# A two-layer convolution kernel: norms with fewer linked steps, another order of VectorE's work, and first pieces that move between engines

## The reference, cut to what matters

```python
# layer 0 (x: 4 x 256 x 64 x 64)
k = conv(x, w1, 7x7, dilation 2, pad 6) + b1            # 256 -> 128 channels
k = conv(k, w2, 1x1) + b2                               # 128 -> 49
attn = softmax(k, axis=1)
x = einsum('bkchw,bkhw->bchw', shifts(x, 49), attn)     # 49 shifted copies, weighted per pixel
# layer 1
h = relu(bn(conv(x, v1, 1x1), g1, c1))                  # 256 -> 64
h = relu(bn(conv(h, v2, 3x3, pad 1), g2, c2))           # 64 -> 64
h = bn(conv(h, v3, 1x1), g3, c3)                        # 64 -> 256
out = relu(h + x)
# bn: mean and variance over batch and pixels, then gamma * (x - mean) / sqrt(var + 1e-5) + beta
```

## Time and profile before

| what | value |
|---|---|
| three runs | 822.93, 823.03, 823.52 us; median 823.03 |
| profiled execution | 823.48 us, its span 821.6 us |
| TensorE busy (matmul) | 787.4 us, 96% of the span |
| VectorE, ScalarE, GpSimd busy | 661.3, 381.8, 353.3 us |
| mean granted clock of TensorE | 0.99 of full |

### The profile page before, as it was taken

How to read it: one execution, slowest core, us unless ns; L and a number is a source line. 1 busy time by engine, 2 the same in 40 slices (tenths; PEclk the granted TensorE clock), 3 DMA queues, 4 the chain that set the end, 5 groups by cost and what they waited for, 6 DMA issues and landing times.

```text
span 821.6 us, 13841 instructions
## 1 busy us (share of the span) xinstructions
PE 787.4 (96%) x4990; PEld 722.5 (88%) x4990; DVE 661.3 (80%) x908; ACT 381.8 (46%) x665; POOL 353.3 (43%) x255
## 2 busy tenths in 40 slices
PE   6989988999999999999999999999998989999996
PEld 2369988999999999999999999999997877777785
DVE  5998998896789689869967896898558766977796
ACT  3632212443453434534434534335336767717497
POOL 3345663483277248525832772385120014415300
PEclk9999999999999999999999999999999989999999
DMA  9951237948894997699588949766877999305398
GB/s 311 326 173 23 53 81 191 242 128 216 181 252 102 246 175 210 167 208 215 133 221 173 252 109 239 157 172 173 194 154 233 284 262 378 133 1 198 148 421 359
DMA packets 250108, 162.17 MB, mean 197 GB/s; under 512 B 191881, under 2 KB 232826, under 8 KB 247226
## 3 DMA queue, kind: packets, MB, share of 16 engines
q1 hardware_dynamic: 241050, 141.31, 65.9%
q10 hardware_dynamic: 8992, 19.99, 7.5%
HBM read 99.48 MB, written 56.36 MB: 190 GB/s over the span
## 4 chain that ended last, share of the span: by engine, by line
PE 73%; DVE 11%; issue 5%; DMA 4%; POOL 3%; ACT 3%; SPq 0%; DVEq 0%; ACTq 0%; POOLq 0%
PE ps L1313 20%; PE ps L1315 20%; PE ps L1314 20%; PE ps L1430 4%; PE ps L1446 3%; PE ps L1480 3%; POOL ring L865 2%; DVE whole L1829 2%; DMA x_dram<-x 1%; DVE logit L1922 1%; DVE wsum L1779 1%; DMA xbuf<-in_x 1%; PE ps L1691 1%; DVE wpart L1779 1%; POOL whole L860 1%
## 5 line engine op out<-in xcount | busy, mean ns | idle before, releaser
L865 POOL TENSOR_TENSOR ring<-whole,ring 128x576 fp32r<-128x576 f32 x112 | 194.1, 1739 | 280.0 <-ACT ring L948 280.0
L1313 PE MATMUL ps<-w_hi,ring 128*128 128x336 f32 x832 | 276.4, 332 | 3.5 <-POOL ring L865 3.5
L1315 PE MATMUL ps<-w_hi,ring 128*128 128x336 f32 x832 | 263.5, 317 | 0.0
L1314 PE MATMUL ps<-w_lo,ring 128*128 128x336 f32 x832 | 262.3, 315 | 0.0
L1313 PEld LDWEIGHTS ps<-w_hi,ring 128*128 128x128 f32 x832 | 158.3, 190 | 9.7 <-issue 6.1
L1314 PEld LDWEIGHTS ps<-w_lo,ring 128*128 128x128 f32 x832 | 158.1, 190 | 0.0
L1315 PEld LDWEIGHTS ps<-w_hi,ring 128*128 128x128 f32 x832 | 157.2, 189 | 0.0
L948 ACT ACTIVATE ring<-whole 128x576 fp32r<-128x576 f32 x112 | 87.1, 782 | 93.8 <-POOL whole L860 52.7
L948 ACT ACTIVATE band_hi<-ps 128x320 fp32r<-128x320 f32 (+1 forms) x128 | 53.1, 418 | 126.8 <-PE ps L1430 119.2
L1313 PE MATMUL ps<-band_hi,xT_hi 128*128 128x224 f32 (+2 forms) x320 | 94.6, 296 | 1.6 <-DVE xT_lo L1732 1.2
L1314 PE MATMUL ps<-band_lo,xT_hi 128*128 128x224 f32 (+2 forms) x320 | 92.3, 288 | 0.0
(11 more groups left out here) (222 smaller groups left out, 1370.9 us busy)
## 6 DMA issues: line engine op xcount, KB each, us to landing
xq<-in_x SPq DMA_DIRECT2D x108, 256.0 KB, 4.7
raw<-bands SPq DMA_DIRECT2D x32, 768.0 KB, 6.8
xbuf<-in_x SPq DMA_DIRECT2D x16, 1024.0 KB, 8.9
x_dram<-x ACTq DMA_DIRECT2D x32, 512.0 KB, 5.7
bands<-wide SPq DMA_DIRECT2D x64, 199.0 KB, 5.0
x1in<-x_dram SPq DMA_DIRECT2D x6, 2048.0 KB, 15.9
out<-x1in SPq DMA_DIRECT2D x12, 1024.0 KB, 4.5
bands<-wide SPq DMA_DIRECT2D x3, 1792.0 KB, 11.3
```

The lines of the kernel that those rows point to most:

```text
L865: pool.tensor_tensor(split(k, 1), positions(whole[:, k % TBUFS, :], 0, 2), split(k, 0).bitcast(F32), ALU.subtract).then_inc(sig_lo_done, 1)
L1313: pe.matmul(dst, l_hi, r_hi_, start=first, stop=False, **kw)
L1314: pe.matmul(dst, l_hi, r_lo_, start=False, stop=False, **kw)
L1315: return pe.matmul(dst, l_lo, r_hi_, start=False, stop=last, **kw)
```

## The change

- **Second pair (VectorE).** `a_of(3)` and `b_of(3)` stand ahead of the last five combines of pair 0 instead of behind them; `signal(20)` ahead of `softmax_top(0)`. In `half(3)` one HALF1 combine moves from part 4 to part 6 and the other two to part 5, behind the first bands.
- **Behind the convolution.** `y_out` is split into `y_add` and `y_stat`; `y_add(g-1, 1)` moves ahead of `xT(g, 2)` and `bandlo(g, 4)`, `y_stat` behind `bandlo(g, 4)`. `xT(13, 0)` moves ahead of the last `softmax_end`, `softmax_max` behind `xT(12, 3)` and `xT(13, 3)`. ScalarE's `x_out(12, 0)` moves behind `xT`.
- **Last projection.** The last half image is projected with eight products of 64 columns that sum in PSUM, so that neither `yhalf` nor the add is needed; `bn_stats` reads PSUM, and ScalarE copies the result out afterwards. Its x goes to DRAM from SyncE's queue instead of ScalarE's, and nine of the thirteen `load_y` are issued behind it.
- **Norms.** EPS and a factor 2 go into the root's bias and scale; the root reads PSUM in BN1; mean*gamma is done beside the root; shift is one instruction from -mean*gamma; scale and shift are not linked. BN2 averages mean and variance in one product. In BN3 the means' products come ahead of the covariance's, and `last(0)` is cut in two around the sums.
- **First pieces.** `step` and `step_lo` of piece 0 move from GpSimd to VectorE; the copies of v3 (`prepare_last`) come behind them; the ReLU of the edge rows of piece 2 moves into piece 1. Dummies: 14 become 9; behind BN2 four `center` products and 5 dummies instead of 16.

The diff, cut to its core:

```diff
@@ SyncE
             store_y(DRAIN)
             load_v()
-            for i in range(STEPS - LAG):
+            for i in range(4):
                 load_y(i)
             store_y(DRAIN + 1)
+            sp.wait_ge(x1_done, 4 * STEPS)
+            sp.dma_start(x1_dram[STEPS - 1][:, :, HALF:SPX].rearrange("b p e -> p b e"),
+                         x1_2[:, :, :]).then_inc(x1_stored[1], 16)
             store_y(DRAIN + 2)
+            for i in range(4, STEPS - LAG):
+                load_y(i)
@@ ScalarE
             prepare(0)
-            yhalf(STEPS - 1, 1)
             x_out(STEPS - 1, 1)
+            act.wait_ge(y1_stat, 2 * STEPS)
+            copy(y1_of(STEPS - 1)[:, 1, :], turn_bank("proj", STEPS - 1, 1)[0:MID1, :]).then_inc(y1_last, 1)
             prepare(1)
-            root(1, BN1_ROOT)
+            act.wait_ge(eps_set, 1)
+            act.wait_ge(bn_pe, 1)
+            root(mv[:, 8:9], ps[:, 7, 0:1], 2.0)
+            for a in range(2):
+                rows = slice(64 * a, 64 * a + 64)
+                copy(v3_hi[rows, a, :], psR[1][rows, C:2 * C]).then_inc(v_hi_done, 1)
@@ ScalarE, h1_part
+                if p != 2:
+                    edges(p)
                 main(0)
...
+                if p == 1:
+                    edges(2)
                 act.wait_ge(left_done, p + 1)
@@ TensorE
-            proj(STEPS - 1, 1)
+            last_proj()
             prepare(1)
...
-            for i in range(14):
+            for i in range(9):
                 pe.matmul(ps[:, spare, 0:P], ident[:, :], ident[:, :], start=True, stop=True)
-            pe.wait_ge(v_lo_done, 8)
-            pe.wait_ge(v_hi_done, 8)
-            pe.wait_ge(vT_done, 2)
+            pe.wait_ge(v_lo_done, 6)
+            pe.wait_ge(v_hi_done, 6)
             pe.wait_ge(borders, 2)
...
             warm(10)
-            average(BN2_MEAN, 0)
-            average(BN2_VAR, 4)
-            warm(16)
+            pe.wait_ge(bn_dve, BN2_MEAN)
+            pe.matmul(ps[:, 7, 0:2], gavg[:, :], mv[:, 0:2], start=True, stop=True).then_inc(bn_pe, 1)
...
+            for k in range(4):
+                centre(k)
+            warm(5)
...
-            last(0)
+            pe.wait_ge(bn_dve, BN3_MEAN)
+            for cb in range(CB):
+                mm = pe.matmul(ps[:, 6, 2 * cb:2 * cb + 2], vT[:, cb * P:(cb + 1) * P], gm[:, 0:2], start=True, stop=True)
+            mm.then_inc(means_ps, 1)
             pe.wait_ge(bn_dve, BN3_COV)
             pe.matmul(ps[:, 3, 0:C], cov[:, :], vT[:, :], start=True, stop=True).then_inc(quad_ps, 1)
-            last(1)
+            last(0, 0)
             pe.wait_ge(bn_dve, BN3_QUAD)
...
             mm.then_inc(sums_ps, 1)
-            for m in range(2, 32):
+            last(0, 1)
+            for m in range(1, 32):
                 last(m)
@@ VectorE, drain
                 bandlo(g, 3)
+                y_add(g - 1, 1)
                 if g > DRAIN:
                     xT(g, 2)
                 bandlo(g, 4)
-                y_out(g - 1, 1)
+                y_stat(g - 1, 1)
@@ VectorE, second pair
                 signal(17)
+                a_of(3)
+                b_of(3)
                 for i in range(C_MHALF + 1, COMBOS):
                     combine(0, i)
-                a_of(3)
-                b_of(3)
                 c_of(2)
+                signal(20)
                 softmax_top(0)
-                signal(20)
                 signal(21)
@@ VectorE, affine
-                link(dve.tensor_scalar(mv[:, 6:8], var, EPS, None, ALU.add))
+                link(dve.tensor_tensor(mv[:, 12:12 + width], mv[:, 2:2 + width], gamma, ALU.mult))
                 dve.wait_ge(bn_act, roots)
-                link(dve.reciprocal(mv[:, 10:12], mv[:, 8:10]))
-                link(dve.tensor_tensor(sc, mv[:, 10:10 + width], gamma, ALU.mult))
-                link(dve.tensor_tensor(mv[:, 12:12 + width], mean, sc, ALU.mult))
-                link(dve.tensor_tensor(sh, beta, mv[:, 12:12 + width], ALU.subtract))
+                link(dve.reciprocal(mv[:, 10:10 + width], mv[:, 8:8 + width]))
+                dve.tensor_tensor(scale[:, i:i + width], mv[:, 10:10 + width], gamma, ALU.mult).then_inc(bn_dve, 1)
+                for j in range(width):
+                    dve.scalar_tensor_tensor(out=shift[:, i + j:i + j + 1], in0=mv[:, 10 + j:11 + j], scalar=mv[:, 12 + j:13 + j],
+                                             in1=beta[:, j:j + 1], op0=ALU.mult, op1=ALU.add).then_inc(bn_dve, 1)
```

More of the change, by code:

```diff
@@ L516, in turn_bank_at @@
             return turns[turn_of[kind, g, i]][3]
+        BN1_MEAN = [b for b in (2, 5, 6) if b not in [turn_bank_at(*t) for t in (("band", STEPS - 1, NT - 1), ("band", STEPS - 1, NT - 2),
+                                                                                ("proj", STEPS - 1, 1))]][0]
         def x_count(g, pt):
@@ L1100, in image_part @@
                     x_hi(image, 0)
-                    x_out(image, 0)
+                    if image < DRAIN - 1:
+                        x_out(image, 0)
                 if part == 12:
@@ L1192, in _, with edges @@
             act.wait_ge(unit_done, len(UNITS) * STEPS)
-            def h1_part(p):
+            def edges(p):
                 n, r0, r1 = PIECES[p]
-                if n >= 2:
-                    act.wait_ge(c2_done, 6 * (n - 1))
-                def main(b):
-                    part = yin[:, 2 * n + b, max(r0, 1):min(r1, SH), :]
-                    act.activation(part, part, ACT.Relu, bias=shift[:, 0:1], scale=scale[:, 0:1]).then_inc(relu1, 1)
                 def edge_row(a, r):
@@ L1219, in h1_part, with main, high @@
                     edge_row(1, SH)
+            def h1_part(p):
+                n, r0, r1 = PIECES[p]
+                if n >= 2:
+                    act.wait_ge(c2_done, 6 * (n - 1))
+                def main(b):
+                    part = yin[:, 2 * n + b, max(r0, 1):min(r1, SH), :]
+                    act.activation(part, part, ACT.Relu, bias=shift[:, 0:1], scale=scale[:, 0:1]).then_inc(relu1, 1)
+                def high(dst, src):
+                    copy(dst, src).then_inc(h1_hi_done, 1)
+                if p != 2:
+                    edges(p)
                 main(0)
@@ L1261, in _ @@
                 c2_copy(j)
-            root(2, BN2_ROOT)
+            act.wait_ge(bn_dve, BN2_ROOT)
+            root(mv[:, 8:9], mv[:, 5:6])
             act.wait_ge(bn_dve, BN2_END)
@@ L1291, in _ @@
             upper(15)
-            root(3, BN3_ROOT)
+            act.wait_ge(bn_dve, BN3_ROOT)
+            root(mv[:, 8:10], gm[:, 12:14])
             act.wait_ge(bn_dve, BN3_END)
@@ L1708, in last @@
                 for b in range(2):
+                    if part == 1 - b:
+                        continue
                     sub = 2 * n + b
@@ L2190, in _ @@
             link(dve.bn_aggr(mv[0:MID1, 0:2], stats1[:, :, :].rearrange("p k e -> p (k e)")))
+            dve.memset(sums[:, 15:16], EPS).then_inc(eps_set, 1)
             dve.wait_ge(bn_loaded, 16 * 12)
@@ L2210, in h1_part @@
                 minus(odd_lo[:, at, r0:r1, :], odd, odd_hi[:, at, r0:r1, :].bitcast(F32)).then_inc(odd_lo_done, 1)
+                if not p:
+                    minus(step[:, r0:r1, :], odd, even).then_inc(step_done, 1)
                 dve.wait_ge(left_edge, p + 1)
@@ L2213, in h1_part @@
                 minus(left_lo[:, at, r0:r1, :], left[:, r0:r1, :], left_hi[:, at, r0:r1, :].bitcast(F32)).then_inc(left_lo_done, 1)
+                if not p:
+                    dve.wait_ge(step_done, 1)
+                    dve.wait_ge(h1_hi_done, STEP + 1)
+                    minus(step_lo[:, at, r0:r1, :], step[:, r0:r1, :], step_hi[:, at, r0:r1, :].bitcast(F32)).then_inc(step_lo_done, 1)
+                    prepare_last()
             def c2_out(j):
```

174 lines of the change are left out of this document (97 added, 77 removed).

## The result

The changed kernel takes 818.11 us (median of 6 runs, 817.34 to 821.49); the kernel before, on the same chip, 823.27 (6 runs, 822.70 to 824.91). The ratio is 0.9941, with an interval of 0.9923 to 0.9960: 5 us faster, where 9 were forecast, and inside the forecast's range by 0.4 us. The profiled execution took 817.85, its span 816.0.

A forecast was written before the change was run, and what follows sets the result against it. A different owner per stage: VectorE in the second pair, first drained images and Gram stage, TensorE in the last. Terms -1.5 - 1.5 - 3.2 - 0.5 - 2.5 + 0.3 = -8.9 led to 814.2 us; range 811.0 to 818.5.

The forecast's parts named there:

- Second pair: Images 2 and 3, 100 to 160 us: reordering VectorE's list makes it net 1.5 us shorter.
- Bounds: 0, if GpSimd's instructions collide with others instead: Second pair: worst case of the -1.5 term, no gain if GpSimd's instructions collide with other ones; best case -3.8.
- For which TensorE then waits a little over 1 us; hidden: Second pair: TensorE waits for ScalarE's late rounding of chunk 20, at no cost, being ahead of VectorE.
- nothing more: Reordering in `half(3)`: removes TensorE's 1.7 us wait but gains no time, as VectorE's later list keeps its length.
- Drained images: Behind the convolution: the earlier `y_add` frees the bank before TensorE asks, saving twice 0.7 us; -1.5.
- Last projection and BN1: Between the convolutions: earlier aggregation, an earlier root and a ScalarE not held by the x store give -3.2 us.
- Rival B: BN1: the x store lands as late as before, ScalarE stays held, gain 1.1 instead of 3.2; 816.3 us; chance 0.12.
- Loads moved behind: Nine y loads, a y store and the last x store, issued later, still arrive in time: 0, bounds 0 and +5.
- First pieces: Start of the second convolution: TensorE's first wait for `odd_lo`, 0.7, goes, the second stays set by ScalarE; -0.5 us.
- BN2: Second norm: shorter chain and fewer dummies bring VectorE's first transposed block from 746.84 to 744.35; -2.5 us.
- BN3: Last stage: TensorE owns it; its new order takes 7.85 us to `last(4)` where it took 7.55; +0.3.
- Rival A: Second pair gains 0 and a low clock in the first pieces costs 1.8 us: 817.5 us; chance 0.2.

The follow-up runs named there:

- 1: The changed kernel with both moves of VectorE's second pair put back (`a_of(3)`/`b_of(3)` and `signal(20)`); ratio 0.9941 to the kernel before.
- 4: The kernel before with only VectorE's new order of the second pair (both moves), nothing else of the change; ratio 1.0014 to the kernel before.
- 2: The changed kernel with only `signal(20)` put back behind `softmax_top`; ratio 0.9923 to the kernel before.
- 3: The changed kernel with only `a_of(3)` and `b_of(3)` put back behind the combines; ratio 0.9947 to the kernel before.
- 5: The changed kernel with ScalarE rounding chunk 20 ahead of pair 0's exponentials instead of behind them; ratio 0.9922 to the kernel before.
- 6: The changed kernel with the combines in `half(3)` put back to their old slots; ratio 0.9947 to the kernel before.
- 9: The changed kernel with `last(0)`'s first half ahead of BN3's means and its second ahead of the sums; ratio 0.9931 to the kernel before.
- 11: The changed kernel with VectorE's old second-pair order and `last(0)`'s halves ahead of BN3's means and sums; ratio 0.9919 to the kernel before.
- 12: The changed kernel with the old second-pair order, `last(0)`'s halves ahead of BN3's means and sums, and `softmax_end(0)` ahead of `signal(21)`; ratio 0.9894, median 815.01 us.
- 7: The changed kernel with all 13 y loads issued in one go again, ahead of the last stores; ratio 0.9966 to the kernel before.
- 8: The changed kernel with 16 dummy products instead of 5 between BN2's averages and the first transposes; ratio 0.9970 to the kernel before.
- 10: The changed kernel without the nine dummies between BN1's averages and the first pieces; ratio 0.9976 to the kernel before.

## Why the prediction was right and where it was not

**The range and the figure.** 818.11 lies inside 811.0 to 818.5, 0.4 from its upper end; the central figure, 814.2, missed it by 3.9. Most stages came out by the steps given. The second pair did not, and one of the prediction's own signs of being wrong came: TensorE's waits as long in sum as before (4.7 for 4.6) and VectorE no earlier.

**Second pair, forecast -1.5, measured +1.2: the step that failed.** The text said that the stretching of `signal(21)` (1.2) and the idle 1.32 before it go. Both went: 0.76 and no wait for GpSimd. It also said that there would be a wait of about 1.0 for the copied rows, with `c_of` and `signal(20)` in front of it; the two take 2.1 longer than it took them for and fill it. GpSimd's signal for chunk 18 was to start 3.8 earlier; counted from `signal(17)` it started 1.3 earlier (108.28 for 109.41), since `a_of` and `b_of` were stretched by 2.2. What it left out is that moved instructions get in GpSimd's way at their new place. VectorE lost 1.1 at `a_of`, 1.1 at `b_of`, 1.0 at `c_of`, 1.05 at `signal(20)` and 1.1 at `wide`: 5.3, against 0.9 + 1.0 + 1.2 saved at the first softmax addition, the subtraction and `signal(21)` and 1.3 of idle time, 4.4. That gives +0.9 of the 1.2. A new idle 0.34 for the exponentials and a `me` that is 0.35 shorter cancel; the remaining 0.3 lies in the hand-overs between instructions. "Bounds: 0, if GpSimd's instructions collide with others instead" saw the mechanism, but took it to be no worse than an even trade, for which it had no reason. The upper bound should have counted each of the moved instructions as meeting one ring step: three of 1.1 are +3.3 against the -1.5. Experiments 1 and 4 show the sign and the size, 2 and 3 that the two moves do not add up.

**Where the wait went.** "For which TensorE then waits a little over 1 us; hidden": the wait was 3.0, since the exponentials came 3.5 later, and it was hidden (5). The reordering in `half(3)`: "nothing more" is right (6); the wait came from another operand.

**Drained images, -1.5:** -1.46. No wait of 0.7 is left from 636 to 660. That the figure agrees this well is in part luck: of the twelve traces with this change seven have 55.9 to 56.1 for the piece, and 3, 6, 9, 11 and 12 have 56.5 to 58.0, where before it was 57.37. In 9, 11 and 12 TensorE waited 1.3, 1.8 and 1.4 for the landing of the bands, and without that they have 56.2; for 3 and 6 the cause stays open.

**Last projection and BN1, -3.2:** -3.35, by the steps given: aggregation at 671.04 (forecast 671.1), root 672.59 (672.65), ReLU 1.07 behind it (1.15). Rival B is refuted for the kernel as changed, and 7 shows its condition: with the loads together ScalarE is held till 672.1, and the gain up to `even_hi` is 1.1 (8.81 for 9.92), as that rival said. The store landed at 666.1, by 666 as forecast. By the rule quoted there (the Trainium skill, DMA: Bandwidth & Descriptors, Queues, rings and completion order) a DMA engine takes turns between the queue rows that have work. The prediction read it as saying that queued loads cost the store little, which the rule does not say; the rows show 12.0 to 12.3 against 4.7 to 6.2, and whether turns alone give that no run here shows.

**Loads moved behind, 0:** no wait for them in the trace.

**First pieces -0.5, BN2 -2.5:** -0.76 and -2.34, to the aggregate's start and from it. That the dummies would have hidden the shorter chain is shown by 8.

**BN3, +0.3:** +0.46 to the fifth tile (8.12 for 7.66, from 767.78 to the 775.44 of the earlier trace rows), for the reason given, and 9 takes it back and 0.26 more. The +0.3 itself rests on a slip: the terms listed add up to 7.65, not 7.85, which would be +0.1 over 7.55. From the first means' product they took 7.88 (761.55 to 769.43), each term a little more than its estimate. Of the +0.9 to the end, 0.4 lies behind the fifth tile, less than the scatter of that piece. In its two longest, 3 (56.1) and 8 (57.2), the granted clock was 0.87 and 0.66 in 765 to 775, where the changed kernel's trace has 1.00: a low stretch can fall on the last stage too, which neither the sum nor a rival counted.

**Rival A** came nearest to the time (817.5), by luck in one of its two parts. The early gain was absent, as it said, but the 1.8 of a low clock on the pieces was not there: the clock did fall, to 0.50 in 674 to 676, beside the dummies. In 7 and 10 it fell on the pieces and cost 0.57 and 0.36 up to the aggregate of BN2 in their traces. What made up the rest is the second pair's +1.2 and the end.

**Sum:** +1.2 for -1.5 is 2.7, the end's 0.6 more than forecast and 0.2 of start-up give 3.5; the other terms gave 0.2 more. -8.9 + 3.3 = -5.6 in the span.

## What to carry to other kernels

When an instruction is moved on VectorE and GpSimd's rows stretch beside it, look up what GpSimd does at the new place, not only what is removed at the old one; a move that fills a hole (12) without meeting GpSimd's work is worth more than one that starts things earlier. Before a chain of small steps is shortened, ask what ends last beside it: in BN2 it was a row of dummies, in BN1 a store beside queued loads. And for edits of 1 us cut the traces at common instructions: pieces with the same code repeated to 0.1 us where the executions of one kernel scatter by 4. But cut more than two: a piece with a landing DMA or a low clock in it scattered by 2 to 3.

## What of the hardware was unexpected

A collision of VectorE and GpSimd is no slowdown by a factor: each of the five stretched instructions of the changed kernel is longer by 0.96 to 1.11 us, whatever its own length (0.75 to 2.55), as if it waited for the rest of one instruction of GpSimd (a ring step of 1.41, or the signal of 1.15 beside `c_of`). It goes the other way too: GpSimd's signal of 1.15 takes 3.40 beside a `c_of` of 2.55 (3). A granted clock of 0.91 in 140 to 160 went with 1.25 us more in each of five traces (1, 8, 10, 11, 12: 64.25 to 64.33 for 63.0), and with none in the nine that had 1.00 there. Where VectorE was the bound it cost nothing: the changed kernel had 0.83 in 120 to 140 and 28.93, and 9, of that order too, 0.91 and 28.98. The x store took 12.0 to 12.3 us with nine more loads queued on the other engine's queue, and 4.7 to 6.2 without them.
